# Attention and feed-forward kernel: pair jobs moved behind the second gate and up group, and a reordered maximum of h

## What is computed

```python
x = x + xattn(layernorm(x), ctx, Wq, Wk, Wv, Wo, bo)   # 8 heads of 64, softmax over 64
x = x + ffn(layernorm(x), w_gate, w_up, w_down)

def act_quant(x):
    scale = 127.0 / clip(max(abs(x), axis=-1), 1e-05)
    return clip(round(x * scale), -128, 127) / scale

def weight_quant(w):
    scale = 1.0 / clip(mean(abs(w)), 1e-05)
    return clip(round(w * scale), -1, 1) / scale

gate = silu(act_quant(x) @ weight_quant(w_gate).T)      # 512 -> 2048
up = act_quant(x) @ weight_quant(w_up).T
out = act_quant(gate * up) @ weight_quant(w_down).T     # 2048 -> 512
```

## Time and profile before

| | us |
|---|---|
| median of 3 runs | 1132.76 |
| lowest and highest run | 1132.17, 1136.36 |
| the profiled execution, its own time | 1135.72 |
| its span in the profile | 1133.9 |
| TensorE (PE) busy | 1071.5 |
| VectorE (DVE) busy | 1003.0 |
| ScalarE (ACT) busy | 744.4 |
| GpSimd (POOL) busy | 497.5 |

### The profile page before, as it was taken

How to read it: one execution, slowest core, us unless ns; L and a number is a source line. 1 busy time by engine, 2 the same in 40 slices (tenths; PEclk the granted TensorE clock), 3 DMA queues, 4 the chain that set the end, 5 groups by cost and what they waited for, 6 DMA issues and landing times.

```text
span 1133.9 us, 17119 instructions
## 1 busy us (share of the span) xinstructions
PE 1071.5 (94%) x5308; PEld 482.7 (43%) x5370; DVE 1003.0 (88%) x2097; ACT 744.4 (66%) x955; POOL 497.5 (44%) x641
## 2 busy tenths in 40 slices
PE   6668999999999999999999999999999999999998
PEld 3323344444344444444444444444444444444443
DVE  5888989978989998988999989889999999998886
ACT  2888657767756676676666666766766666665543
POOL 1046544556544445455443454454444444444110
PEclk9769999999999999999999999999999999999999
DMA  9798653564355454354455544544555544554334
GB/s 349 218 257 163 110 116 75 89 136 103 73 118 122 103 117 112 79 112 107 99 106 118 117 106 94 104 108 85 115 117 120 101 106 103 121 108 93 72 73 98
DMA packets 355962, 133.79 MB, mean 118 GB/s; under 512 B 332448, under 2 KB 332960, under 8 KB 355360
## 3 DMA queue, kind: packets, MB, share of 16 engines
q1 hardware_dynamic: 355872, 132.70, 53.1%
HBM read 34.08 MB, written 16.78 MB: 45 GB/s over the span
## 4 chain that ended last, share of the span: by engine, by line
PE 38%; DVE 19%; issue 6%; POOL 4%; ACT 4%; DMA 1%; SPq 0%; ACTq 0%; DVEq 0%; POOLq 0%
PE ps L1327 17%; PE ps L1346 8%; PE ps L1266 4%; PE ps L1267 4%; PE ps L1269 4%; DVE hm L1040 3%; DVE FF L1032 2%; DVE FF L1085 2%; POOL rs L653 2%; DVE bns L1018 1%; POOL MV L698 1%; DVE hm L1036 1%; ACT FF L818 1%; DVE xr L1024 1%; DVE am L1041 1%
## 5 line engine op out<-in xcount | busy, mean ns | idle before, releaser
L1327 PE MATMUL ps<-wgT,FF 128*128 128x512 bf16 x1024 | 262.9, 379 | 1.6 <-ACT FF L818 1.0
L1327 PE MATMUL ps<-wW,FF 128*128 128x512 bf16 x1024 | 262.9, 379 | 1.6 <-DVE FF L1032 1.6
L1346 PE MATMUL ps<-wW,FF 128*128 128x512 bf16 x962 | 218.7, 379 | 9.5 <-DMA FF<-FF 4.8
L827 ACT ACTIVATE FF<-FF,c 128x1024 int16<-128x1024 f32 x128 | 141.1, 1141 | 124.1 <-DVE c L1045 121.5
L818 ACT ACTIVATE FF<-ps,sgu 128x512 f32<-128x512 f32 x256 | 173.4, 680 | 63.5 <-PE ps L1327 62.0
L1032 DVE TENSOR_TENSOR FF<-FF,ps 128x512 f32<-128x512 f32 x256 | 173.4, 681 | 38.0 <-ACT FF L818 18.9
L679 POOL TENSOR_TENSOR AT<-AT,rd 128x512 f32<-128x512 f32 x64 | 67.4, 1053 | 298.3 <-DVE rd L1077 295.1
L1346 PEld LDWEIGHTS ps<-wW,FF 128*128 128x128 bf16 x1024 | 99.7, 98 | 128.4 <-issue 7.2
L1327 PEld LDWEIGHTS ps<-wW,FF 128*128 128x128 bf16 x1024 | 99.7, 98 | 123.9 <-DVE FF L1032 4.9
L1327 PEld LDWEIGHTS ps<-wgT,FF 128*128 128x128 bf16 x1024 | 98.8, 98 | 124.9 <-issue 3.2
L667 POOL TENSOR_TENSOR xhl<-xn,xhl 128x512 f16<-128x512 f32 x64 | 74.1, 1158 | 75.4 <-ACT xhl L834 75.4
(11 more groups left out here) (142 smaller groups left out, 1730.7 us busy)
## 6 DMA issues: line engine op xcount, KB each, us to landing
xr<-in_x SPq DMA_DIRECT2D x64, 256.0 KB, 2.8
out<-xr SPq DMA_DIRECT2D x64, 256.0 KB, 2.3
FF<-in_L_ffn_w_gate SPq DMA_DIRECT2D x4, 1024.0 KB, 13.4
wW<-in_L_ffn_w_up SPq DMA_DIRECT2D x4, 1024.0 KB, 14.2
FF<-in_L_ffn_w_down SPq DMA_DIRECT2D x4, 1024.0 KB, 6.1
FF<-FF SPq DMA_TRANSPOSE x192, 3.2
MV<-in_L_xattn_Wq SPq DMA_DIRECT2D x1, 1024.0 KB, 5.7
MV<-in_L_xattn_Wo SPq DMA_DIRECT2D x1, 1024.0 KB, 12.3
```

What stands on the lines that cost most here:

```text
L827: eng.activation(q16h[:, 1024 * z:1024 * z + 1024], h[:, t % 2, 1024 * z:1024 * z + 1024], ACT.Copy, scale=c2[:, t % W:t % W + 1]).then_in ...
L1327: mm = eng.matmul(bank[n % 2][:, :].rearrange("p (o f) -> p o f", o=4), qxT[:, i % 2, k, :], w[:, 4 * f:4 * f + 4, k, :], start=(k == 0), ...
L1346: mm = eng.matmul(y_bank(i)[:, :], hT[:, i % 2, c, :], wdT[:, c, :], start=(c == 0), stop=(c == 15))
```

## The change

Two things change. The fractions in JOB_F are new, so that pair_X comes behind the second gate_up group, the first j_wide and j_hi behind exp, the second pair behind the third silu and quant_x, and both j_lo between x_lo and p_norm. And h_part now scales its half's maximum itself, and waits for its reduce to do so; h_max combines the second half's maximum with that in one instruction, t2 = max(hm1 · sgu, hm2), and the instruction that took the larger of the two maxima is gone.

```diff
-        JOB_F = (0.266, (0.324, 0.399), (0.388, 0.623))
+        JOB_F = (0.462, (0.562, 0.630), (0.576, 0.632))
...
             def h_part(i):
                 eng.wait_ge(v_h, 4 * i + 2)
-                eng.tensor_reduce(hm[:, 0:1], h[:, i % 2, 0:1024], AX_X, ALU.max, apply_absolute_value=True)
+                link(eng.tensor_reduce(hm[:, 0:1], h[:, i % 2, 0:1024], AX_X, ALU.max, apply_absolute_value=True))
+                eng.tensor_scalar(hm[:, 2:3], hm[:, 0:1], sgu[:, 1, i % W:i % W + 1], EPS, ALU.mult, ALU.max)
 
             def h_max(i):
                 eng.wait_ge(v_h, 4 * i + 4)
                 link(eng.tensor_reduce(hm[:, 1:2], h[:, i % 2, 1024:2048], AX_X, ALU.max, apply_absolute_value=True))
-                link(eng.tensor_tensor(am[:, 1, i % W:i % W + 1], hm[:, 0:1], hm[:, 1:2], ALU.max))
-                link(eng.tensor_scalar(t2[:, i % W:i % W + 1], am[:, 1, i % W:i % W + 1], sgu[:, 1, i % W:i % W + 1], EPS,
+                link(eng.tensor_scalar(t2[:, i % W:i % W + 1], hm[:, 1:2], sgu[:, 1, i % W:i % W + 1], hm[:, 2:3],
                                        ALU.mult, ALU.max))
```

## The result

The changed kernel takes **1120.55 us** (median of 4 runs, 1117.95 to 1123.34), against 1132.47 for the kernel before beside it. The ratio is 0.9884, 95% interval 0.9849 to 0.992: 13.1 us gained on 1132.47. I had forecast 1123.6, a gain of 9.2, in a range from 1120.5 to 1130.5. The direction and the place were right.

What follows compares the result with a forecast made beforehand. TensorE's matmuls bound plain steps; job steps also stall on L1024. Gains of 9.7 (place) − 1.1 (down's wait) + 0.6 (h chain) = 9.2 us, from the median 1132.76, gave 1123.6 us, range 1120.5 to 1130.5.

Steps and rivals of the forecast that it cites:

- 23.7 us stand over it in 16 job steps: Steps with a pair job for batches 4 to 7 last 1.48 us each over TensorE's 15.54 us plain step.
- 9.7 us go with the place: Moving pair_X behind the second group removes TensorE's wait for L1024; the job's own 0.88 us per step stay.
- Final is late by VectorE's own queue: Final (L1024), which reads bank pY before the job overwrites it, waits behind VectorE's h chain, not for TensorE.
- Down waits 0.14 us in each r < 4 step: Down projection waits for ScalarE's second read, ending near 8.65 us against 8.66; eight such jobs give back 1.1 us.
- The h chain is worth 0.6 us outside the job steps: Shorter VectorE chain counts only in the opening and last tile: 0.6 us, bounds −0.5 to 3.
- the bounds most at hand: Down's wait 0 to 3 us and h chain 0 to 2 us, giving the forecast's own range, 1121.5 to 1126.
- rival 2: The h chain also shortens opening and tail by 3 us, giving 1121.2 us; chance 0.08.
- Rival 1: ScalarE's second read runs 0.45 us later in all 16 job steps, so down waits: 1129.7 us; chance 0.18.
- Rivals 3 and 4: GpSimd holds lengthen the job step: two of 0.35 give 1130.3 (chance 0.09), two of 0.65 give 1139.9 (chance 0.07).
- the ring: Dependency loop through GpSimd from one second j_hi to the next, counted at 16.2 us, under the step's 16.4.

Runs made afterwards that it cites:

- the place alone: New JOB_F fractions of the pair jobs with the old h chain, against the kernel before: 1123.01 us, ratio 0.9894.
- the late read: The changed kernel with ScalarE's second read of the job's banks moved behind the fourth silu: 1131.51 us, ratio 1.0001 to the kernel before.

## Why the prediction was right and wrong

- *TensorE's own work bounds the plain step; 23.7 us stand over it in 16 job steps.* Right: 124.32 us for eight plain steps in every kernel with undisturbed jobs.
- *9.7 us go with the place.* Right: the series fell by 4.7 and 4.7, 9.4 us, and as much with the place alone.
- *Final is late by VectorE's own queue.* Right: shortening that queue alone shortened the wait, from 8.7 to 2.8 us.
- *Down waits 0.14 us in each r < 4 step, 1.1 us given back.* Wrong in size: nothing is given back. The first read, quant_x and the second read each start about 0.1 us before the end of what stands ahead of them; after small lags elsewhere 0.23 is to be subtracted, where I subtracted 0.13. The durations sum to 4.96, not 5.00, and the release is 0.10. My sum gave 8.65, the trace 8.52. The mechanism is real: 0.04 us further and it begins, and the late read paid it in full.
- *The h chain is worth 0.6 us outside the job steps, since "most opening steps show TensorE busy".* This is the step that failed. It is worth about 2.6, of which 1.8 arise up to the third down and 0.8 at the end. TensorE's busy share was 90% and more there too, yet its steps had no even pace before about 345 us. I priced L1041 at the 0.20 of the tail, while it took 0.89 and 1.09 us in two of the first three tiles, and I gave that rival 0.08. At the end I counted the last tile alone, where four of the last six are on the chain. The bound that I had set (3 us) was right, the value inside it was not.
- The range by the bounds most at hand begins at 1132.76 − (9.7 + 2) = 1121.1, not at 1121.5 as I wrote.
- With the terms as measured: 9.4 − 0 + 2.6 = 12.0 us, 2.8 more than the forecast's 9.2. The ratios give 13.1 (interval 9.1 to 17.1), 12.8 (11.3 to 14.4) and 15.5 (12.5 to 18.5): the third lies above what the traces add up to, and that rest is not explained. A gain of 12.0 would have been 1120.8 us, inside the range, whose lower edge had room for it by rival 2; that the first ratio lies beyond it is in part the scatter of the runs.
- *Rival 1 (down takes the wait over)* didn't come, by 0.04 us. *Rival 2 (the h chain gives 3 us)* is in its mechanism what came. *Rivals 3 and 4 (a ring through GpSimd)*: the ring did not set the step. It is close: x_norm waited 0.16 us for rstd and the second silu still had 0.21 of idle time ahead of it. GpSimd was held at one place in it, d_scale, and only in the steps with r < 4; its groups in the job steps, after and before:

```profile
L660 POOL TENSOR_SCALAR sd<-t,wst 128x1 f32<-128x1 f32 x7 | 4.4, 624 | 0.0
```

```profile
L660 POOL TENSOR_SCALAR sd<-t,wst 128x1 f32<-128x1 f32 x8 | 2.5, 308 | 0.0
```

The first row is of the changed kernel, the second of the one before. d_scale meets VectorE's casts (L1050) now, and takes 0.85 to 0.86 us in the four steps with r < 4 and 0.31 or 0.32 in the others. The rivals had two holds of 0.35 or more; there is one of 0.55 (0.86 − 0.31). The Trainium skill, SBUF — State Buffer, section Who interferes with whom, has it that of the two engines the one that issues second is blocked. That one is held for as long as the other works agrees with these rows and with L1085, which is 480 ns where it was 1394; which issued second they don't show, since d_scale's record starts at 460.08 and the cast's at 460.17.

## What to carry to other kernels

An engine at its own pace hides every other; find the few steps where it isn't, and price the work by its distance to the two things around it: what it waits for and who waits for it. Moving a job on one engine means moving its readers too, and a place between two waits can be right by 0.04 us, so count starts, not durations. A cut on a chain that repeats for each tile is worth something only in the tiles where the bounding engine waits for that chain, and there it is worth the size that the instruction has in those tiles, not its mean. Here all of the opening's gain is there by the third down, and four tiles at the end account for most of the rest. Look at such tiles one by one before calling a cut free.

## What I had not expected of the hardware

A 128x1 tensor_tensor on VectorE took 159 ns with GpSimd idle, 642 in plain steps, where it started while p_lo ran on GpSimd, and up to 1087 in the opening. With the place alone it was 159 ns in the job steps and 581 in the plain ones after them (a mean: seven of about 640, and one of 159 from the last job step):

```profile
L1041 DVE TENSOR_TENSOR am<-hm 128x1 f32<-128x1 f32 x7 | 1.1, 159 | 0.2
...
L1041 DVE TENSOR_TENSOR am<-hm 128x1 f32<-128x1 f32 x8 | 4.7, 581 | 0.3
```

A 128x1 tensor_scalar with two per-partition scalars from memory takes 273 ns (L1042 after), with one of them 214 (L1042 before, L1037 after). And in the kernel with only TensorE's place moved, the gate group behind the 2.69 us of idle time ran its matmuls 0.42 us apart in place of 0.216: the granted clock of 576 to 582 us was 0.72 of full speed, so part of that stretch ran at 1.2 GHz, while 570 to 576 had 1.00.
